# A four-layer decoder kernel: the first layer's cross attention in steps of two heads

## The chip, the cores and the metric

The kernel runs on one core of a Trainium2 chip, as one program. The metric is the device time of one execution in microseconds. Five engines work side by side and meet through semaphores: TensorE (PE, with its weight loads shown apart as PEld), VectorE (DVE), ScalarE (ACT), GpSimd (POOL) and SyncE (SP), which only issues DMAs. Each engine works through its own instructions in order.

## The reference

Sixteen sequences of 112 tokens with 256 features go through four layers, each with self attention (or a state-space block) and cross attention to a context of 375 rows. All is float32. What matters here is the second half of the first layer, cut to its core:

```
# D, H, DH = 256, 16, 64; x: (16, 112, 256), context: (16, 375, 256)
xn, cn = layer_norm(x, gamma_ca), layer_norm(context, gamma_ctx)
q = heads(xn @ w_q) * DH ** -0.5          # 16 heads of 64
k, v = split(cn @ w_kv)                   # one head of keys and values for all queries
p = softmax(q @ k.T, axis=-1)             # (16 heads, 112, 375) for each sequence
attn = merge_heads(p @ v) @ w_out
ff = (silu(gate) * value) @ w_ff2         # gate, value = split(xn @ w_ff1)
x = x + attn + ff
```

## The kernel before

The layers run one after the other. `layer0` (L814) takes the sequences in pairs: 8 turns, the last one written apart, since it prepares no next pair. Each engine has its own program for a turn (`turn`), written in the same order of steps on all: self attention, a middle part (`between_phases`), cross attention, `turn_ending`. No planner decides anything; the order is written out by hand, with lags.

**Items.** Queries lie with their features on the partitions: heads 2t and 2t+1 in the lower and the upper 64 partitions of `qT[:, j, t, :]`. Seen as rows (`rows_of`), the 8 head pairs of 112 tokens are 896 columns per sequence, cut into 7 tiles of 128. An item of the cross attention is one tile and one side: `cross_at(k)` gives sequence j, tile m and side a, so there are 2 x 7 x 2 = 28 items in a turn, 224 in all, and items k and k+1 (k even) are the two sides of one tile. The keys are kept twice, in `ckz[:, j, 0, :]` with zeros in the upper and in `ckz[:, j, 1, :]` with zeros in the lower 64 partitions. So a score product contracts all 128 partitions (`cross_q`, `cross_k`), and the zeros pick the side.

**Steps of one item** (class `Columns`, L227):

- *scores* (L303, product at L311): TensorE, 128 x 375 into one of two PSUM banks of the ring `S`. A float32 product shows as two MATMUL records.
- *maxima* (L447): VectorE reads the bank and makes the negated maximum of each row.
- *exps* (L409): ScalarE reads the bank, writes the exponentials to a slot of `p` in SBUF, and their sums. The end of it frees the bank.
- *inverses* (L456) and *scale* (L365): VectorE's reciprocal of the sums, and the scaling of `p` in place.
- *turns* (L319): TensorE transposes `p` in three parts of 125 keys into one of two banks of the ring `TR`.
- *turned* (L389): ScalarE copies them into a slot of `pT`.
- *values* (L341): TensorE multiplies by the values, for two items at once: item k-1 into the lower and item k into the upper 64 partitions of an output bank, 6 products in 12 records. Every 8 items or so VectorE copies the output bank (L429).

**Order.** `lagged` (L187) runs a loop over steps n on every engine. At step n TensorE does the turns of item n-3, the scores of item n, and for odd n the values of items n-5 and n-4. ScalarE does the copy of item n-3, then the exponential of item n. VectorE does the maximum of item n, then the inverse and scaling of item n-1, then what output copy is due.

**Beside the attention** each step may have other work (`cross_side`), behind the attention's own on each engine. On TensorE: at steps 0 and 2 the products of the last two gates of the feed-forward (8 records of 128x224), at 3 the values of the second context, at 25 the transposes of the next tokens, at 28 to 30 keys, the output products of the first sequence, values and queries. On ScalarE the tanh of each gate (L1153); on VectorE its hidden part (L1281, L1283), the statistics of the next tokens at step 8 (`measure_x`) and their centring at step 12.

The class has a second way for items whose scores get a bias (`by_probs`, used in the third and the fourth layer). There VectorE takes the scores out of the bank with one custom instruction (L444), which adds the bias, writes the negated sums to `p` and keeps their minimum, and a second record that reads the minimum out. ScalarE then takes the exponential from `p` (L406), with scale -1. The bank is free after VectorE's instruction. Since the custom instruction carries no wait, a memset of one element (`take_wait`, L692) waits ahead of it. The self attention of the first layer (`grouped`) has its own form of this.

Of the kernel before, what the change touches and what calls it, by code (L numbers as in the profile page):

```python
# [9 lines left out]
NB, T, D, S2 = 16, 112, 256, 375  # L10
PAIR = 2
# [188 lines left out]
class Part:  # L200


    def __init__(self, name, items, dh, rows, q, k, val, ready, val_ready, place, out, bias=None, grouped=False, sides=2, tiles=CT,
                 turned_by="act", emptied_by="dve", scaled_by="dve", ring=None):
        self.name, self.items, self.dh, self.rows, self.q, self.k, self.val, self.ready = name, items, dh, rows, q, k, val, ready
        self.val_ready, self.place, self.out, self.bias, self.grouped, self.sides, self.ring = val_ready, place, out, bias, grouped, sides, ring
        self.turned_by, self.emptied_by, self.scaled_by = turned_by, emptied_by, scaled_by
        self.keys, self.tiles = (T, 1) if grouped else (CP, tiles)
        self.n = G if grouped else 1
        self.by_probs = bias is not None  # L210
        self.scored_by = "dve" if self.by_probs else "act"

    def bursts(self, k):
        return self.grouped or k % self.sides == self.sides - 1
# [12 lines left out]
class Columns(Attention):  # L227
# [74 lines left out]
    def tensor(self, pe, i, parts, ident, between=None):  # L302
        S, TR, p, pT = self.S, self.TR, self.p, self.pT  # L303

        def scores(ph, k):
            m = ph.first + k
            for sem, count in S.free(i, m, *ph.ready(k)):
                pe.wait_ge(sem, count)
            width = ph.keys * ph.tiles
            for g in range(ph.n):  # L310
                last = pe.matmul(S.bank(m)[:ph.rows, g * width:(g + 1) * width], ph.q(k, g), ph.k(k, g), start=True, stop=True)  # L311
            last.then_inc(S.full.sem, 1)

        def turns(ph, k):
            m = ph.first + k
            for sem, count in TR.free(i, m, self.scaled[ph.scaled_by].this(ph.scaled0 + k)):
                pe.wait_ge(sem, count)
            for g in range(ph.n * ph.tiles):
                last = pe.transpose(TR.bank(m)[:ph.keys, g * ph.rows:(g + 1) * ph.rows], p[:ph.rows, m % self.p_slots, g * ph.keys:(g + 1) * ph.keys],  # L319
                                    ident[:ph.rows, :ph.rows])  # L320
            last.then_inc(TR.full.sem, 1)

        def values(ph, k):
            if not ph.bursts(k):
                return
            m, P, w = ph.first + k, ph.ring or self.P, ph.rows
            job, column = ph.place(k)
            together = [k] if ph.grouped else list(range(k - ph.sides + 1, k + 1))
            ready = [TR.got(ph.first + n) for n in together] + ph.val_ready(k)
            for sem, count in P.free(i, job, *ready) if ph.opens(k) else counts(i, *ready):  # L330
                pe.wait_ge(sem, count)
            bank = P.bank(job)
            if ph.grouped:
                for g in range(ph.n):
                    a, c = g % ph.sides, g // ph.sides
                    last = pe.matmul(bank[a * ph.dh:(a + 1) * ph.dh, c * w:(c + 1) * w], ph.val(k, g, 0), pT[:ph.keys, m % self.pT_slots, g * w:(g + 1) * w],
                                     start=True, stop=True)
            else:
                for t in range(ph.tiles):
                    for a, n in enumerate(together):  # L340
                        last = pe.matmul(bank[a * ph.dh:(a + 1) * ph.dh, column:column + w], ph.val(n, 0, t),  # L341
                                         pT[:ph.keys, (ph.first + n) % self.pT_slots, t * w:(t + 1) * w], start=(t == 0), stop=(t == ph.tiles - 1))
            last.then_inc(P.full.sem if ph.closes(k) else self.values.sem, 1)

        self.lagged(parts, [(self.lag_t, turns), (0, scores), (self.lag_v, values)], between)
# [39 lines left out]
    def scalar(self, act, i, parts, between=None, amid=None):  # L385
        S, p, nm, sums = self.S, self.p, self.nm, self.sums
# [23 lines left out]

        def turned(ph, k):
            if ph.turned_by == "act":
                self.turned_copy(act, i, ph, k, copy)

        def outputs(ph, k):
            if ph.emptied_by == "act" and ph.closes(k):
# [8 lines left out]
    def vector(self, dve, i, parts, between=None, amid=None):  # L425
        S, p, nm, sums, rs = self.S, self.p, self.nm, self.sums, self.rs
# [32 lines left out]

        def turned(ph, k):  # L460
            if ph.turned_by == "dve":
                self.turned_copy(dve, i, ph, k, copy)

        def outputs(ph, k):
            if ph.emptied_by == "dve" and ph.closes(k):
# [348 lines left out]
def layer0(nc, c, x_in, context, x_out, lines, w, prefetch, next_x):  # L814


    DH, HT = 64, H * 64 // 128
# [3 lines left out]
    with ctx:  # L821
        def sb(name, *shape):
            return ctx.enter_context(nc.sbuf_tensor("l0_" + name, list(shape), F32))
# [7 lines left out]
        ktmp, kz = sb("ktmp", 128, 2, TP), sb("kz", 128, PAIR, 2, T)  # L831
# [3 lines left out]
        OT = sb("OT", 128, PAIR, 8, T)  # L835
        cx, cT = sb("cx", CP, PAIR, CT, D), sb("cT", 128, PAIR, KT, S2)
        ckz, cv = sb("ckz", 128, PAIR, 2, S2), sb("cv", CP, PAIR, CT, DH)
        st, mv = sb("st", 128, 6, 6), sb("mv", 128, 3, 6, 2)
        ve, rstd = sb("ve", 128, 6), sb("rstd", 128, 3, 6)
        cos, sin = c.rope[:, 0:TP], c.rope[:, TP:2 * TP]  # L840
# [12 lines left out]
        rows_of = qT[:, :, :, :].rearrange("p j n t -> p j (n t)")  # L853
        OT_of = OT[:, :, :, :].rearrange("p j n t -> p j (n t)")
        LAG_VALUES = 4
        ROWS, TILES = 128, HT * T // 128
# [14 lines left out]
        def cross_at(k):  # L871
            return k // (2 * TILES), k % (2 * TILES) // 2, k % 2
# [9 lines left out]

        def cross_q(k, g):
            j, m, a = cross_at(k)
            return rows_of[:, j, ROWS * m:ROWS * (m + 1)]

        def cross_place(k):
            j, m, a = cross_at(k)
# [2 lines left out]
        def cross_out(k):  # L891
# [3 lines left out]
        own = Part("s", PAIR * H // G, DH, T, own_q, lambda k, g: kz[:, own_at(k)[0], g % 2, :], lambda k, g, t: v[:, own_at(k)[0], :], own_ready, own_values_ready,  # L895
                   lambda k: (f"sO{own_at(k)[0]}{own_at(k)[1]}", 0), lambda k: OT_of[:, own_at(k)[0], own_at(k)[1] * 2 * T:(own_at(k)[1] + 1) * 2 * T],
                   bias=lambda k: wide(c.causal[:T, :], 1, G), grouped=True, scaled_by="pool")
        cross = Part("c", PAIR * 2 * TILES, DH, ROWS, cross_q, lambda k, g: ckz[:, cross_at(k)[0], cross_at(k)[2], :], lambda k, g, t: cv[:, cross_at(k)[0], t, :],
                     cross_ready, cross_values_ready, cross_place, cross_out)

        beside_own = {s: [(f"f{s}", "dve")] for s in range(8)}
        beside_own[8] = [("cT00", "act"), ("cT01", "act"), ("y0", "dve")]
# [61 lines left out]
        def _(pool):  # L964
# [18 lines left out]
            for s in (rooted, pool_steps.raises):  # L983
                pool.sem_inc(s.sem, COMING)
            A.scaled["pool"].prime(pool)
            for a in (kz[:, :, :, :], ckz[:, :, :, :]):
                pool.memset(a, 0.0).then_inc(zeroed, 1)
            pool.wait_ge(zeroed, 2)
            pool_steps.start(-1, COMING)
# [260 lines left out]
        def _(dve):  # L1250
# [9 lines left out]
            def center(i, n, sources, outs):  # L1260
                m, size = NORMS.index(n), sources[0].shape[0]
                dve.wait_ge(rooted.sem, rooted.count(i, m))
                for a, (src, out) in enumerate(zip(sources, outs)):
                    last = dve.tensor_scalar(out, src, mv[:size, m, a, 0:1], rstd[:size, m, a:a + 1], ALU.subtract, ALU.mult)
                last.then_inc(normed.sem, 1)
# [119 lines left out]
            lines.scale(dve, banks[0:2])  # L1385
            measure_context(-1)
            center(-1, "c", context_rows, context_rows)
            with dve.Fori(0, TURNS - 1) as i:
                turn(i, True)
            turn(TURNS - 1, False)  # L1390
# [1979 lines left out]
```

## Time and profile before

| | us |
|---|---|
| median of 3 runs | 3669.17 (3668.32 to 3670.8) |
| the profiled execution | 3673.39 |
| its span | 3671.6 |
| TensorE busy | 3435.7 (94%) |
| TensorE weight loads | 2524.7 (69%) |
| ScalarE busy | 1912.8 (52%) |
| VectorE busy | 1881.6 (51%) |
| GpSimd busy | 397.5 (11%) |

The span is what the profile covers of the execution. Busy times are unions of an engine's records; matmuls are pipelined, so that a record (0.48 us for 128x375) is longer than the time from one start to the next. For TensorE the times from start to start are the ones to add up. In a timeline, instructions of one kind that follow each other are one row: start, length of the whole, engine, line, operation, output and input, count, and in brackets the idle time ahead of it with what ended it.

### The profile page before, as it was taken

Reading aid. Unit: us, or ns where it says so; the run is one execution under the profiler, and the core shown is the slowest. Engines: PE = TensorE matmul, PEld = TensorE weight load, DVE = VectorE, ACT = ScalarE, POOL = GpSimd, SP = SyncE. Lnnn points to the kernel's source line nnn. Section 1 sums busy time; section 2 is a strip of 40 time slices with the busy share of each in tenths; the row PEclk is TensorE's granted clock in tenths of the full one; section 3 lists DMA queues with packets and bytes.
Section 4 is the critical chain, followed back from the end, with each engine's and each line's share of the span. In section 5 each row is a group of like instructions: output and inputs, shape, how many; then the busy total and the mean of one; then the engine's idle time right before and its main releaser. Section 6 shows DMA issues by size and latency. Waiting matters only on the chain. (4 is left out here: it accounts for less than half of the span.)

```text
span 3671.6 us, 67713 instructions
## 1 busy us (share of the span) xinstructions
PE 3435.7 (94%) x21748; PEld 2524.7 (69%) x21748; DVE 1881.6 (51%) x5735; ACT 1912.8 (52%) x5549; POOL 397.5 (11%) x488
## 2 busy tenths in 40 slices
PE   8999999999997999999988999999999998798887
PEld 6778778778775666666656666667666675565665
DVE  3654654644644444455544554455445444656655
ACT  3553543544544555656644554555555454366666
POOL 2101101101102111001101000000000000211111
PEclk9999999999998999999999999999999999899999
DMA  6000000000004000000001000000000000000000
GB/s 207 4 12 15 4 12 15 4 12 15 4 3 150 14 8 5 13 13 13 13 6 55 9 8 11 8 12 9 8 15 9 8 10 14 12 18 22 13 27 5
DMA packets 58462, 75.11 MB, mean 20 GB/s; under 512 B 6752, under 2 KB 55584, under 8 KB 57024
## 3 DMA queue, kind: packets, MB, share of 16 engines
q1 hardware_dynamic: 58176, 71.45, 6.3%
q8 instruction: 160, 2.62, 0.3%
q14 instruction: 126, 1.03, 0.1%
HBM read 64.04 MB, written 7.40 MB: 19 GB/s over the span
## 5 line engine op out<-in xcount | busy, mean ns | idle before, releaser
L161 PE MATMUL l_bank<-l_xT,weights_of_layers_and 128*128 128x224 f32 x2816 | 616.7, 371 | 14.8 <-ACT l_xT L1143 8.0
L161 PEld LDWEIGHTS l_bank<-l_xT,weights_of_layers_and 128*128 128x128 f32 x2816 | 542.4, 199 | 58.4 <-ACT l_xT L1143 8.7
L389 ACT ACTIVATE l_pT<-l_bank 125x336 f32<-125x336 f32 (+2 forms) x736 | 347.6, 472 | 321.1 <-PE l_bank L319 310.8
L319 PEld LDWEIGHTS l_bank<-identity,l_p 112*125 112x125 f32 (+2 forms) x2336 | 332.1, 177 | 198.6 <-issue 112.0
L319 PE MATMUL l_bank<-identity,l_p 112*125 112x112 f32 (+2 forms) x2336 | 387.7, 278 | 36.2 <-ACT l_p L363 30.8
L406 ACT ACTIVATE l_p<-l_p,l_nm 112x375 f32<-112x375 f32 x384 | 233.2, 607 | 234.3 <-DVE l_nm L444 233.0
L161 PE MATMUL l_bank<-weights_of_layers_and,l_cT 128*125 128x256 f32 (+2 forms) x960 | 303.8, 454 | 13.6 <-DVE l_queries_or_hidden L1845 9.3
L161 PE MATMUL l_bank<-l_cT,weights_of_layers_and 128*128 128x375 f32 x832 | 304.0, 494 | 0.0
L710 POOL TENSOR_TENSOR l_ve<-l_mv,eps 112x2 f32<-112x2 f32 (+1 forms) x89 | 17.3, 195 | 2438.8 <-DVE l_mv L704 2438.8
L402 ACT ACTIVATE l_p<-l_p,l_nm 112x112 f32<-112x112 f32 x512 | 192.2, 377 | 149.4 <-DVE l_nm L440 130.8
L341 PEld LDWEIGHTS l_bank<-l_pT,l_cv 125*64 125x64 f32 (+1 forms) x3648 | 162.8, 130 | 137.0 <-issue 97.0
L444 DVE CUSTOM_DVE_ANT_0 l_p<-l_bank,weights_of_layers_and 112x375 f32<-112x375 f32 x256 | 139.3, 544 | 202.4 <-issue 122.0
L161 PEld LDWEIGHTS l_bank<-weights_of_layers_and,l_cT 128*125 128x125 f32 x960 | 160.4, 189 | 101.0 <-issue 53.6
L341 PE MATMUL l_bank<-l_pT,l_cv 125*64 125x112 f32 (+2 forms) x3648 | 225.0, 272 | 2.0 <-ACT l_pT L389 1.8
L161 PEld LDWEIGHTS l_bank<-l_cT,weights_of_layers_and 128*128 128x128 f32 x832 | 155.2, 194 | 100.2 <-issue 16.3
L365 DVE TENSOR_SCALAR l_p<-l_p,l_rs 112x375 f32<-112x375 f32 (+1 forms) x480 | 199.5, 416 | 17.1
L311 PE MATMUL l_bank<-l_ckT,l_qz 128*112 128x375 f32 x512 | 203.2, 480 | 0.2
L640 DVE TENSOR_REDUCE l_nm<-l_bank 112x1 f32<-112x375 f32 x256 | 140.1, 547 | 123.4 <-PE l_bank L554 121.3
L554 PE MATMUL l_bank<-l_ckT,l_queries_or_hidden 128*112 128x375 f32 x512 | 201.2, 479 | 0.0
L562 PEld LDWEIGHTS l_bank<-identity,l_p 112*125 112x125 f32 (+1 forms) x1024 | 140.2, 175 | 85.0 <-ACT l_p L619 27.8
L562 PE MATMUL l_bank<-identity,l_p 112*125 112x112 f32 (+1 forms) x1024 | 171.3, 280 | 7.8 <-ACT l_pT L623 5.6
L409 ACT ACTIVATE l_p<-l_bank,l_nm 128x375 f32<-128x375 f32 x224 | 128.5, 574 | 96.1 <-DVE l_nm L447 95.4
(255 smaller groups left out, 5887.4 us busy)
## 6 DMA issues: line engine op xcount, KB each, us to landing
l_cT<-in_ctx_turned SPq DMA_DIRECT2D x32, 375.0 KB, 3.5
l_cx<-in_ctx SPq DMA_DIRECT2D x16, 375.0 KB
context_rows<-in_ctx_reversed SPq DMA_DIRECT2D x16, 375.0 KB
tokens<-x_after_layer SPq DMA_DIRECT2D x25, 224.0 KB, 2.5
x_after_layer<-l_z SPq DMA_DIRECT2D x24, 224.0 KB, 2.4
weights_of_layers_and<-bias_lines_kept SPq DMA_DIRECT2D x1, 2625.0 KB, 15.6
weights_of_layers_and<-in_L_xattn_w_fused SPq DMA_DIRECT2D x1, 2048.0 KB, 10.9
weights_of_layers_and<-in_L_xattn_w_ff SPq DMA_DIRECT2D x1, 2048.0 KB, 12.8
```

The source lines that it names most:

```text
L161: last = pe.matmul(out, left, right, start=(k == 0), stop=(k == len(pairs) - 1))
L311: last = pe.matmul(S.bank(m)[:ph.rows, g * width:(g + 1) * width], ph.q(k, g), ph.k(k, g), start=True, stop=True)
L319: last = pe.transpose(TR.bank(m)[:ph.keys, g * ph.rows:(g + 1) * ph.rows], p[:ph.rows, m % self.p_slots, g * ph.keys:(g + 1) * ph.keys], i ...
L341: last = pe.matmul(bank[a * ph.dh:(a + 1) * ph.dh, column:column + w], ph.val(n, 0, t), pT[:ph.keys, (ph.first + n) % self.pT_slots, t * w ...
L365: eng.tensor_scalar(own, own, self.rs[:r, c:c + 1], None, ALU.mult).then_inc(self.scaled["dve"].sem, 1)
L389: return act.activation(out, src, ACT.Copy)
L402: last = act.activation(own, own, ACT.Exp, bias=nm[:r, c + g:c + g + 1], accum_out=sums[:r, c + g:c + g + 1])
L406: act.activation(own, own, ACT.Exp, bias=nm[:r, c:c + 1], scale=-1.0, accum_out=sums[:r, c:c + 1]).then_inc(self.probs.sem, 1)
L444: dve.tensor_tensor_reduce(p[:r, m % self.p_slots, 0:S2], S.bank(m)[:r, 0:S2], ph.bias(k), -1.0, 3.0e38, ALU.add, ALU.min, nm[:r, c:c + 1] ...
L554: last = pe.matmul(S.bank(m)[:T, g * width:(g + 1) * width], ph.q(k, g), ph.k(k, g), start=True, stop=True)
L562: last = pe.transpose(TR.bank(m)[:ph.keys, g * T:(g + 1) * T], p[:, m % self.p_slots, g * ph.keys:(g + 1) * ph.keys], ident[:T, :T])
L640: dve.tensor_reduce(nm[:, n, k:k + 1], S.bank(m)[:T, 0:S2], AX.X, ALU.max, negate=True).then_inc(self.neg_max.sem, 1)
```

## The change

The cross attention of the first layer goes in steps of two items. Each product contracts only the 64 partitions that hold its side (`cross_q` and the new `cross_k`). On TensorE the scores of items n and n+1 are issued together at even n, behind the waits of both, and the turns of two items together at even n; ScalarE's copies are paired in the same way. The part gets a bias of zeros, so it now takes the `by_probs` way: VectorE takes the scores out, ScalarE's exponential reads SBUF. GpSimd fills the zeros at the start. Other parts keep `abreast=1`, which issues what was issued before.

```diff
+    def abreast_of(self, k):
+        n = self.abreast
+        return range(k - n + 1, k + 1) if k % n == n - 1 else ()
...
         def scores(ph, k):
-            m = ph.first + k
-            for sem, count in S.free(i, m, *ph.ready(k)):
-                pe.wait_ge(sem, count)
+            own = ph.abreast_of(k + ph.abreast - 1)
             width = ph.keys * ph.tiles
-            for g in range(ph.n):
-                last = pe.matmul(S.bank(m)[:ph.rows, g * width:(g + 1) * width], ph.q(k, g), ph.k(k, g), start=True, stop=True)
-            last.then_inc(S.full.sem, 1)
+            for n in own:
+                for sem, count in S.free(i, ph.first + n, *ph.ready(n)):
+                    pe.wait_ge(sem, count)
+            for n in own:
+                for g in range(ph.n):
+                    last = pe.matmul(S.bank(ph.first + n)[:ph.rows, g * width:(g + 1) * width], ph.q(n, g), ph.k(n, g), start=True, stop=True)
+                last.then_inc(S.full.sem, 1)
 
         def turns(ph, k):
-            m = ph.first + k
-            for sem, count in TR.free(i, m, self.scaled[ph.scaled_by].this(ph.scaled0 + k)):
-                pe.wait_ge(sem, count)
...
+            for n in ph.abreast_of(k):
+                m = ph.first + n
+                for sem, count in TR.free(i, m, self.scaled[ph.scaled_by].this(ph.scaled0 + n)):
+                    pe.wait_ge(sem, count)
...
         def turned(ph, k):
             if ph.turned_by == "act":
-                self.turned_copy(act, i, ph, k, copy)
+                for n in ph.abreast_of(k):
+                    self.turned_copy(act, i, ph, n, copy)
...
+        no_bias = sb("no_bias", 128, S2)
...
         def cross_q(k, g):
             j, m, a = cross_at(k)
-            return rows_of[:, j, ROWS * m:ROWS * (m + 1)]
+            return rows_of[64 * a:64 * a + 64, j, ROWS * m:ROWS * (m + 1)]
+
+        def cross_k(k, g):
+            j, m, a = cross_at(k)
+            return ckz[64 * a:64 * a + 64, j, a, :]
...
-        cross = Part("c", PAIR * 2 * TILES, DH, ROWS, cross_q, lambda k, g: ckz[:, cross_at(k)[0], cross_at(k)[2], :], lambda k, g, t: cv[:, cross_at(k)[0], t, :],
-                     cross_ready, cross_values_ready, cross_place, cross_out)
+        cross = Part("c", PAIR * 2 * TILES, DH, ROWS, cross_q, cross_k, lambda k, g, t: cv[:, cross_at(k)[0], t, :],
+                     cross_ready, cross_values_ready, cross_place, cross_out, bias=lambda k: no_bias[:, :], abreast=2)
...
-            for a in (kz[:, :, :, :], ckz[:, :, :, :]):
+            for a in (kz[:, :, :, :], ckz[:, :, :, :], no_bias[:, :]):
                 pool.memset(a, 0.0).then_inc(zeroed, 1)
...
+            dve.wait_ge(zeroed, 3)
             with dve.Fori(0, TURNS - 1) as i:
```

## Rows read from the trace of the kernel before

**Rows 1.** Windows of the first layer's cross attention, one turn; columns in the first line.
```profile
core 0: us, PE busy (x) PEld busy (x) DVE busy (x) ACT busy (x) POOL busy (x), PEclk, DMA share, GB/s
367.70:424.70 57.00, 56.77 (x398) 41.50 (x397) 35.87 (x107) 32.91 (x94) 0.89 (x2) 1.00 0.00 1
```

**Rows 2.** Timeline of TensorE in that stretch: start, length, engine, line, names, count.
```profile
376.93 0.88 PE L341 MATMUL l_bank<-l_pT,l_cv 125*64 125x128 f32 x12
377.74 0.59 PE L319 MATMUL l_bank<-identity,l_p 128*125 128x128 f32 x3
378.17 0.80 PE L311 MATMUL l_bank<-l_ckz,l_qT 128*128 128x375 f32 x2
378.80 0.49 PE L319 MATMUL l_bank<-identity,l_p 128*125 128x128 f32 x3
379.13 0.80 PE L311 MATMUL l_bank<-l_ckz,l_qT 128*128 128x375 f32 x2
379.85 0.88 PE L341 MATMUL l_bank<-l_pT,l_cv 125*64 125x128 f32 x12
```

**Rows 3.** Timeline of ScalarE and VectorE in the same stretch.
```profile
398.34 0.48 ACT L389 ACTIVATE l_pT<-l_bank 125x384 f32<-125x384 f32 x1
398.75 0.57 ACT L409 ACTIVATE l_p<-l_bank,l_nm 128x375 f32<-128x375 f32 x1
...
400.11 0.55 DVE L447 TENSOR_REDUCE l_nm<-l_bank 128x1 f32<-128x375 f32 x1 [0.87 <-PE l_bank L311]
```

**Rows 4.** Timeline of the fourth layer: scores taken out with a bias.
```profile
3182.42 0.48 PE L311 MATMUL l_bank<-l_ckT,weights_of_layers_and 128*112 128x375 f32 x1
...
3183.04 0.06 DVE L692 MEMSET l_scratch<- 1x1 f32 x1 [0.48 <-PE l_bank L311]
...
3183.57 0.16 DVE L456 RECIPROCAL l_rs<-l_sums 112x1 f32<-112x1 f32 x1
...
3183.69 0.61 ACT L406 ACTIVATE l_p<-l_p,l_nm 112x375 f32<-112x375 f32 x1 [0.54 <-DVE l_nm L444]
```

**Rows 5.** Timeline of VectorE at the third layer's end: reciprocal, scaling, memset.
```profile
3088.71 0.16 DVE L456 RECIPROCAL l_rs<-l_sums 112x1 f32<-112x1 f32 x1
3088.90 0.41 DVE L365 TENSOR_SCALAR l_p<-l_p,l_rs 112x375 f32<-112x375 f32 x1
3089.26 0.06 DVE L692 MEMSET l_scratch<- 1x1 f32 x1
```

**Rows 6.** Timeline of the start of the first layer's cross attention.
```profile
364.68 3.19 PE L161 MATMUL l_bank<-l_xT,weights_of_layers_and 128*128 128x224 f32 x16
...
367.71 0.79 PE L311 MATMUL l_bank<-l_ckz,l_qT 128*128 128x375 f32 x2
367.99 0.36 ACT L1153 ACTIVATE l_th<-l_bank 128x224 f32<-128x224 f32 x1 [1.16 <-PE l_bank L161]
...
369.11 0.54 DVE L447 TENSOR_REDUCE l_nm<-l_bank 128x1 f32<-128x375 f32 x1
...
375.24 0.80 PE L311 MATMUL l_bank<-l_ckz,l_qT 128*128 128x375 f32 x2
```

**Rows 7.** Timeline around steps 8, 12 and 24 of the same stage.
```profile
382.58 0.42 DVE L365 TENSOR_SCALAR l_p<-l_p,l_rs 128x375 f32<-128x375 f32 x1
...
383.86 0.52 DVE L447 TENSOR_REDUCE l_nm<-l_bank 128x1 f32<-128x375 f32 x1
...
389.22 0.73 DVE L1264 TENSOR_SCALAR l_xhat<-tokens,l_mv,l_rstd 112x256 f32<-112x256 f32 x2
...
405.12 0.80 PE L311 MATMUL l_bank<-l_ckz,l_qT 128*128 128x375 f32 x2
```

**Rows 8.** Timeline: TensorE where it starts again, turns and values.
```profile
384.48 0.42 DVE L365 TENSOR_SCALAR l_p<-l_p,l_rs 128x375 f32<-128x375 f32 x1
...
385.04 0.56 PE L319 MATMUL l_bank<-identity,l_p 128*125 128x128 f32 x3 [0.23 <-DVE l_p L365]
...
3664.46 0.45 ACT L389 ACTIVATE l_pT<-l_bank 125x336 f32<-125x336 f32 x1 [0.38 <-PE l_bank L319]
...
3664.96 0.49 PE L341 MATMUL l_bank<-l_pT,l_cv 125*32 125x112 f32 x11 [0.60 <-ACT l_pT L389]
```

More of the change, by code:

```diff
@@ L203, in __init__ @@
     def __init__(self, name, items, dh, rows, q, k, val, ready, val_ready, place, out, bias=None, grouped=False, sides=2, tiles=CT,
-                 turned_by="act", emptied_by="dve", scaled_by="dve", ring=None):
+                 turned_by="act", emptied_by="dve", scaled_by="dve", ring=None, abreast=1):
+        self.abreast = abreast
         self.name, self.items, self.dh, self.rows, self.q, self.k, self.val, self.ready = name, items, dh, rows, q, k, val, ready
@@ L305, in scores @@
         def scores(ph, k):
-            m = ph.first + k
-            for sem, count in S.free(i, m, *ph.ready(k)):
-                pe.wait_ge(sem, count)
+            own = ph.abreast_of(k + ph.abreast - 1)
             width = ph.keys * ph.tiles
-            for g in range(ph.n):
-                last = pe.matmul(S.bank(m)[:ph.rows, g * width:(g + 1) * width], ph.q(k, g), ph.k(k, g), start=True, stop=True)
-            last.then_inc(S.full.sem, 1)
-        def turns(ph, k):
-            m = ph.first + k
-            for sem, count in TR.free(i, m, self.scaled[ph.scaled_by].this(ph.scaled0 + k)):
-                pe.wait_ge(sem, count)
[L318 to L321, printed above, removed]
+            for n in own:
[5 more added lines that the diff above has]
+                last.then_inc(S.full.sem, 1)
+        def turns(ph, k):
+            for n in ph.abreast_of(k):
+                m = ph.first + n
+                for sem, count in TR.free(i, m, self.scaled[ph.scaled_by].this(ph.scaled0 + n)):
+                    pe.wait_ge(sem, count)
+                for g in range(ph.n * ph.tiles):
+                    last = pe.transpose(TR.bank(m)[:ph.keys, g * ph.rows:(g + 1) * ph.rows], p[:ph.rows, m % self.p_slots, g * ph.keys:(g + 1) * ph.keys],
+                                        ident[:ph.rows, :ph.rows])
+                last.then_inc(TR.full.sem, 1)
         def values(ph, k):
@@ L461, in turned @@
             if ph.turned_by == "dve":
-                self.turned_copy(dve, i, ph, k, copy)
+                for n in ph.abreast_of(k):
+                    self.turned_copy(dve, i, ph, n, copy)
         def outputs(ph, k):
```

## The prediction

> **What bounds the kernel now.** I read the page first: TensorE is busy for 94% of the span, the other engines for about half. Then the windows of the stretch that the change touches, the cross attention of the first layer: of the 57 us that it takes in one turn, 56.77 us are TensorE work, at a granted clock of 1.00, while VectorE has 35.9 us and ScalarE 32.9 us [rows 1]. Then the timeline of TensorE. A pair of heads (items m and m+1) costs it 2.92 us. Two score products take 0.63 us each (378.17 to 378.80), two groups of turns 0.43 and 0.33 (377.74 to 378.17, 378.80 to 379.13), the values 0.81 with the change of mode behind them (376.93 to 377.74), and the change ahead of them 0.09 (0.72 from 379.13 to the values of the next pair, less 0.63): 1.26 + 0.76 + 0.81 + 0.09 = 2.92 [rows 2]. Nothing waits on TensorE. VectorE sits idle for 0.87 us ahead of a reduce, until a score product ends [rows 3]. So TensorE is the bound, and there are 14 pairs in each of 8 turns. The question is whether it stays the bound.
>
> **Scores on half the rows.** Each item's product now contracts 64 partitions, one item on the lower and one on the upper half, into two banks. No row shows two products in different row halves. Below, they overlap wholly, and a pair costs 0.63; above, not at all, 1.26. The nearest rows are the values, which sit in two column halves: 12 records take 0.81 including the change, where 12 records of the turns' rate (0.33 for 3) would take 1.32 [rows 2]. They overlap in twos, so I take 0.63.
>
> The Trainium skill (TensorE: Matmul & The Clock Gate, Part 3) has such products run side by side at about 4 ns each. That is the same 0.63, so by it the sum stands.
>
> The change of mode into the row halves is new. It lies between nothing and the whole 0.35 that a change into and out of the column halves costs (0.09 ahead, 0.81 less 6 x 0.11 behind, and 0.10 on the first turn). I take 0.15 into it, and keep 0.09 into the values. TensorE's own work per pair becomes 0.76 + 0.15 + 0.63 + 0.09 + 0.81 = 2.44, 0.48 less than now.
>
> **The new order.** TensorE issues turns(m-4), turns(m-3), scores(m), scores(m+1), values(m-4, m-3). Before, turns and scores alternated, and values(m-4, m-3) came after turns(m-2) and scores(m+1). There are still two score banks, and the scores of a pair wait until both are free. ScalarE issues copy(m-4), copy(m-3), exp(m), exp(m+1), VectorE take(m), inverse(m-1), take(m+1), inverse(m). A take is a memset, the custom add-and-minimum and its accumulator read; an inverse is reciprocal and scaling.
>
> **The takes.** The last score's start plus its 0.48 gives its end; the memset starts 0.14 later, for 3182.42 + 0.48 = 3182.90 against 3183.04. The next VectorE instruction starts 0.53 after the memset, and the exponential of that item 0.65 after it, so a take is over at 0.61 [rows 4]. An inverse holds VectorE for 0.55 (3088.71 to 3089.26) [rows 5]. The exponential from SBUF holds ScalarE for 0.61 [rows 4], a copy for 0.41 (398.34 to 398.75), with 0.48 to its end [rows 3]. VectorE has 2 x (0.53 + 0.55) = 2.16 of work per pair and ScalarE 2 x (0.61 + 0.41) = 2.04. By busy time alone everyone fits under 2.44. The order is what does not.
>
> The Trainium skill (TensorEngine Tiling (Array Packing), PSUM Bottleneck) warns that tiling speeds up TensorE but not the emptying of PSUM, and that both engines should share the emptying. By that rule this change, which gives the scores to VectorE alone, would gain less than 0.48 a pair; the loops below are how that would look here.
>
> **Two loops.** The short one goes through the banks. From take(m+1) over: TensorE restarts (0.15, as a turn after a scaling: 384.48 + 0.42 to 385.04 [rows 8]), change 0.15, scores 0.32 + 0.48 = 0.80, then 0.14 + 0.53 for take(m+2), 0.55 for inverse(m+1), 0.61 for take(m+3): 2.93 for one pair. The long one goes through the copies, since on ScalarE the copies of m-2 and m-1 are queued behind exp(m+1). From take(m+1) over: 0.04 + 0.61 for the exponential, 0.41 + 0.48 for two copies, 0.05 to the values (3664.46 + 0.45 to 3664.96 [rows 8]), values 0.81, turns(m), turns(m+1) 0.76, change 0.15, scores 0.80, and 0.14 + 0.53 + 0.55 + 0.61 until take(m+5) is over. That is 5.94 for two pairs, 2.97 each. Behind the values wait the turns and the scores of the pair after. So what ended last, TensorE at 2.92, is replaced by a chain of 2.97, and TensorE idles for about half a microsecond per pair. From pair 4 to pair 26 there are 11 steps: 11 x 0.05 = +0.55 us per turn.
>
> **Start of the stage.** At steps 0 and 2 the last two gate products of the feed-forward stand beside the attention. On VectorE their hidden part is queued behind take(0) and ahead of take(1), and scores(2) and (3) now need take(1). The chain is: scores 0.63, back to full rows 0.20 (between nothing and the 0.26 behind the values), gate products 1.51 (half of the 16 from 364.68 to 367.71), 0.28 until the tanh, 1.12 from the tanh to VectorE's next instruction, take(1) 0.61, restart and change 0.30 [rows 6]. That is 4.65, and the same again with step 2, so scores(4) start 9.30 after scores(0). Now it is 7.53 (367.71 to 375.24) [rows 6]. The loss is +1.77 us per turn. Until now TensorE went on with scores(1) while VectorE did the hidden part.
>
> **Insertions on VectorE.** The statistics of the next tokens at step 8 push the next instruction on the scores from 0.36 after a scaling (3088.90 to 3089.26) to 1.28 (382.58 to 383.86), so +0.92; the centring at step 12 holds VectorE for 0.73 [rows 5, 7]. Now TensorE absorbs most: from scores(4) to scores(24) it takes 29.88 us (375.24 to 405.12), 10 x 2.92 and 0.68 more [rows 6, 7]. In the new order both lie inside the loops, 1.65 in place of 0.68: +1.0 us in the seven turns that have a next one. The output copies fall into the time in which VectorE waits for scores; nothing for them. The transposes of the next tokens at step 25 cost TensorE the same on both sides.
>
> **At nothing:** the fill of the zero bias (0.2 to 0.5 us of GpSimd at the very start, ahead of a wait that ends on VectorE), the third count that VectorE waits for once, and the end of the turn, where 7 us of output products on TensorE cover what is late. If that cover is short, it costs 0.3 per turn.
>
> **The sum.** 8 x (0.55 + 1.77) + 7 x 1.0 = 18.6 + 7.0 = +25.6 us. The profiled execution took 3673.39 (span 3671.6 and 1.8 around it), so 3699.0 in its terms; it was 4.2 above the median of the runs, 3669.17, so the median should come to 3694.8, that is 3695 us.
>
> **Rivals.**
> *The row halves don't overlap* (0.15). TensorE then needs 2.44 + 0.63 = 3.07 per pair, above both loops: 11 x 0.10 more than forecast, and 2 x 0.63 in the chain of the start, 2.4 per turn, +19: 3714. For it: fp32 products come as two passes, and no row proves row halves. Against it: the column halves of the values.
> *TensorE stays the bound* (0.12), the one that ends faster. It decides at 2.44: the long loop would have to be under 4.88, 1.06 less than my rows give, for instance if exponentials, copies and restarts overlap more behind one another. Then 11 x 0.48 = 5.3 less; the start at TensorE's own 6.99 (2 x (0.63 + 0.15 + 0.20) + 2 x 1.51 + 1.25 for the context values + 0.76) instead of 7.53; insertions hidden, 0.68 less: 6.5 per turn, -52: 3617. For it: 2.16 and 2.04 of work under 2.44. Against: every link of the long loop has a row, and four of them (exponential, copies, values, turns) are long ones in a fixed order.
> *Gain and loss cancel* (0.09). The mode changes cost nothing and the gates at the start are half hidden: 2.8 per pair gives -1.3, the start +0.9, the insertions +0.5: 3669 to 3670.
> *The clock falls* (0.03). TensorE would wait for a sixth of the stage with half its rows idle. Its 2.44 at the 1.2 GHz level would be near 4.9, against 2.92: 2 x 14 x 8 = +220, 3890. Against: the clock stays at 1.00 wherever this stage waits now.
>
> **Numbers.** My forecast has 0.61, with its own range 3682 to 3710: both loops move by 0.08 a pair with the mode change, the start by 0.4 a turn. The range 3660 to 3722 leaves out the faster rival, the clock and the upper part of the first rival. No change is within 0.2% (7 us), which is what a measurement of this kernel can tell. Faster: 0.12 and a fifth of the third rival, 0.14. Same: the rest of the third, 0.07. Slower: 0.79.
>
> **What would show it.** Right: pairs of score records of 128x375 with the stationary from 64 rows starting within 0.02 us of each other; a pair step of 2.9 to 3.1 us, TensorE idle ahead of the values until a ScalarE copy, and ahead of scores(2) and (4) until VectorE's take; exponentials in the first layer from SBUF at 0.61 us; scores(0) to scores(4) near 9.3 us; a granted clock of 1.00. Wrong: a pair step near 2.5 with TensorE unbroken; score records one behind the other; or a stage under 57 us in one turn.

## The result, and the profile after

The kernel after takes 3684.27 us (median of 7 runs, 3682.54 to 3684.64), the kernel before 3671.07 beside it (7 runs, 3668.32 to 3672.28). The ratio is 1.0035, with a 95% interval of 1.0024 to 1.0046: slower by 13.2 us. The profiled execution took 3684.27 with a span of 3682.5, 10.9 more than the span before, at a mean granted clock of 0.977 (before 0.976).

The page has TensorE busy for 92% of the span in place of 94%: it now has less to do, and waits instead.

Windows of the kernel after in the first layer: a whole turn, from its first score product to that of the next turn, then the score products 0 to 26 (the last pair) of one of the first seven turns and of the last.

```profile
core 0: us, PE busy (x) PEld busy (x) DVE busy (x) ACT busy (x) POOL busy (x), PEclk, DMA share, GB/s
371.12:507.47 136.35, 126.01 (x858) 102.81 (x857) 71.90 (x263) 64.44 (x204) 15.88 (x22) 1.00 0.03 11
371.12:413.76 42.64, 35.87 (x290) 24.49 (x289) 30.49 (x144) 27.60 (x77) 0.95 (x2) 1.00 0.01 1
1054.65:1095.48 40.83, 35.44 (x286) 24.17 (x285) 28.90 (x137) 27.61 (x77) 0.00 (x0) 1.00 0.00 1
```

The kernel before, with the same columns: a whole turn, one that is 1.68 longer because the granted clock is lower in it, and the same two stretches of score products.

```profile
367.71:501.55 133.84, 131.16 (x857) 107.01 (x857) 71.37 (x207) 63.87 (x204) 15.79 (x22) 1.00 0.04 11
232.19:367.71 135.52, 132.84 (x857) 108.35 (x856) 71.36 (x207) 63.87 (x204) 15.80 (x22) 0.99 0.03 11
367.71:408.39 40.68, 40.45 (x289) 28.11 (x289) 30.48 (x92) 27.63 (x80) 0.89 (x2) 1.00 0.00 1
1040.43:1080.08 39.65, 39.65 (x285) 28.11 (x285) 28.44 (x85) 27.31 (x79) 0.00 (x0) 1.00 0.00 1
```

Compare turns at the same clock: 133.84 against 136.35, +2.51 us. Between scores(0) and scores(26) TensorE's work fell by 4.58 us (40.45 to 35.87), and the stretch grew by 1.96 (40.68 to 42.64): 6.77 us of the stretch are now idle, where 0.23 were.

Groups of instructions of the first layer in the kernel after: who makes whom wait (busy us, mean ns, then idle time ahead and its releaser).

```profile
L453 DVE CUSTOM_DVE_ANT_0 l_p<-l_bank,l_no_bias 128x375 f32<-128x375 f32 x224 | 121.9, 544 | 68.1 <-PE l_bank L327 37.1 <-issue 30.7
L318 PE MATMUL l_bank<-l_ckz,l_qT 64*128 64x375 f32 x448 | 101.5, 530 | 21.0 <-DVE l_nm L453 21.0
L349 PE MATMUL l_bank<-l_pT,l_cv 125*64 125x128 f32 x1344 | 98.1, 281 | 40.7 <-ACT l_pT L397 38.7 <-issue 0.7
```

TensorE waits twice: 21.0 us ahead of scores, for VectorE's take, and 40.7 us ahead of values, for ScalarE's copy. That is 7.7 us per turn. Both are the waits that the prediction named.

Timeline of the start of the stage after, answering to [rows 6].

```profile
371.12 0.90 PE L318 MATMUL l_bank<-l_ckz,l_qT 64*128 64x375 f32 x4
371.95 1.78 PE L161 MATMUL l_bank<-l_xT,weights_of_layers_and 128*128 128x224 f32 x8
...
374.24 0.39 DVE L1296 SCALAR_TENSOR_TENSOR l_u<-l_th,l_bank 128x224 f32<-128x224 f32 x1 [1.26 <-ACT l_th L1168]
...
374.97 0.54 DVE L453 CUSTOM_DVE_ANT_0 l_p<-l_bank,l_no_bias 128x375 f32<-128x375 f32 x1
375.58 0.90 PE L318 MATMUL l_bank<-l_ckz,l_qT 64*128 64x375 f32 x4 [1.84 <-DVE l_nm L453]
...
380.08 0.90 PE L318 MATMUL l_bank<-l_ckz,l_qT 64*128 64x375 f32 x4
```

VectorE has the instruction that uses the tanh (L1296) queued behind take(0), waits 1.26 us for the tanh, and only then makes take(1), for which TensorE has stood for 1.84 us. scores(0) to scores(4) take 8.96 us (371.12 to 380.08), where they took 7.53 [rows 6].

TensorE some pairs later, after, answering to [rows 2].

```profile
383.58 0.90 PE L318 MATMUL l_bank<-l_ckz,l_qT 64*128 64x375 f32 x4
...
385.22 1.03 PE L327 MATMUL l_bank<-identity,l_p 128*125 128x128 f32 x6
386.18 0.90 PE L318 MATMUL l_bank<-l_ckz,l_qT 64*128 64x375 f32 x4
387.62 0.88 PE L349 MATMUL l_bank<-l_pT,l_cv 125*64 125x128 f32 x12 [0.54 <-ACT l_pT L397]
...
389.75 0.90 PE L318 MATMUL l_bank<-l_ckz,l_qT 64*128 64x375 f32 x4 [0.40 <-DVE l_nm L453]
```

The four passes of two items take 0.90 us to the end of the record, where two passes of one item took 0.80 [rows 2]. The pair steps are 2.60 and 3.57. The second holds VectorE's statistics: TensorE waits 0.40 us for the take that stands behind them.

The loops undisturbed, in the last turn, after. The steps are 2.66 (1078.39 to 1081.05) and 3.04 (to 1084.09), 2.85 on average.

```profile
1080.34 0.54 DVE L453 CUSTOM_DVE_ANT_0 l_p<-l_bank,l_no_bias 128x375 f32<-128x375 f32 x1
1080.92 0.61 ACT L414 ACTIVATE l_p<-l_p,l_nm 128x375 f32<-128x375 f32 x1 [0.30 <-DVE l_nm L453]
1081.05 0.90 PE L318 MATMUL l_bank<-l_ckz,l_qT 64*128 64x375 f32 x4
1081.53 0.85 ACT L397 ACTIVATE l_pT<-l_bank 125x384 f32<-125x384 f32 x2
1081.99 0.54 DVE L453 CUSTOM_DVE_ANT_0 l_p<-l_bank,l_no_bias 128x375 f32<-128x375 f32 x1 [0.58 <-issue]
1082.01 0.06 DVE L702 MEMSET l_scratch<- 1x1 f32 x1
1082.43 0.88 PE L349 MATMUL l_bank<-l_pT,l_cv 125*64 125x128 f32 x12 [0.48 <-ACT l_pT L397]
```

This is the long loop: take until 1080.88, exponential 0.61, two copies 0.85, values, turns. It also shows where the forecast of the takes was too long: scores start at 1081.05 and their records end at 1081.95, the take starts at 1081.99. The record of the memset lies beside it (1082.01), not ahead of it.

### The profile page after: what moved, and what is told of

Read it like the earlier page. It is cut to its first block and busy times, and to the rows that moved or that the text cites. A ratio compares the mean times of both kernels' runs of the same rounds, so it can differ in the third digit from the quotient of the medians.

```text
span 3682.5 us, 67747 instructions
## 1 busy us (share of the span) xinstructions
PE 3390.8 (92%) x21748; PEld 2487.4 (68%) x21748; DVE 1885.3 (51%) x6183; ACT 1918.2 (52%) x5549; POOL 398.4 (11%) x489
## 5 line engine op out<-in xcount | busy, mean ns | idle before, releaser
L414 ACT ACTIVATE l_p<-l_p,l_nm 112x375 f32<-112x375 f32 (+1 forms) x608 | 369.4, 608 | 346.9 <-DVE l_nm L453 341.6
L397 ACT ACTIVATE l_pT<-l_bank 125x336 f32<-125x336 f32 (+2 forms) x736 | 334.6, 470 | 316.3 <-PE l_bank L327 313.8
L327 PEld LDWEIGHTS l_bank<-identity,l_p 112*125 112x125 f32 (+2 forms) x2336 | 318.7, 177 | 167.1 <-issue 106.7
L327 PE MATMUL l_bank<-identity,l_p 112*125 112x112 f32 (+2 forms) x2336 | 370.9, 278 | 34.0 <-ACT l_p L371 30.8
L629 ACT ACTIVATE l_p<-l_bank,l_nm 112x375 f32<-112x375 f32 x256 | 147.0, 574 | 51.4 <-DVE l_nm L650 49.4
## 6 DMA issues: line engine op xcount, KB each, us to landing
weights_of_layers_and<-in_L_xattn_w_fused SPq DMA_DIRECT2D x1, 2048.0 KB, 10.9
weights_of_layers_and<-in_L_xattn_w_ff SPq DMA_DIRECT2D x1, 2048.0 KB, 13.2
```

Of the source, the lines that this page charges most:

```text
L397: return act.activation(out, src, ACT.Copy)
L414: act.activation(own, own, ACT.Exp, bias=nm[:r, c:c + 1], scale=-1.0, accum_out=sums[:r, c:c + 1]).then_inc(self.probs.sem, 1)
L629: act.activation(slot[:, 0:S2], S.bank(m)[:T, 0:S2], ACT.Exp, bias=nm[:, n, k:k + 1], accum_out=sums[:, n, j, h:h + 1]).then_inc(S.emptier ...
```

## The experiments

Each kernel was timed beside the kernel before, which stood at 3670 to 3672 us throughout. "Steps" are the times from scores(0) to scores(2), from there to scores(4) and so on, in a profiled turn that has a next one. For the kernel after they begin 4.46, 4.51. Ratios are to the kernel before, with 95% intervals.

The traces allow a finer comparison than the totals. Of the second to the sixth turn, those in which the granted clock is 1.00 throughout take the same time within 0.03 us in each kernel (but for one turn of the side-work experiment, 1.0 longer). What differs from trace to trace besides the work is the number of short stretches (3.4 us) at half the granted clock, and the time behind the first layer, where the code is the same in all of them. Each row is one profiled execution:

| kernel | turn at full clock, us | stretches at half clock, first layer after 100 us | from the last turn's second output products to the end, us |
|---|---|---|---|
| before | 133.84 | 3 | 2578.1 |
| after | 136.35 | 1 | 2572.8 |
| half rows alone | 140.79 | 4 | 2577.3 |
| pairs, full rows | 136.87 | 1 | 2572.1 |
| take alone | 133.90 | 4 | 2572.0 |
| pairs, no take | 140.47 | 2 | 2574.3 |
| side work odd | 132.36 | 2 | 2575.9 |
| gates odd | 134.03 | 5 | 2574.8 |
| before, side work odd | 133.19 | 0 | 2577.4 |
| turns apart | 133.24 | 0 | 2575.9 |
| both | 130.05 | 1 | 2573.8 |

The last column spreads over 6 us with nothing changed, so a gap of a few microseconds between two profiled executions says nothing about the stage.

### Half rows without the pairs and without the take

The kernel before with only the operands of the score products changed (stationary and moving from 64 rows). Against the kernel after, bias and steps of two are taken out:

```
-                     cross_ready, cross_values_ready, cross_place, cross_out, bias=lambda k: no_bias[:, :], abreast=2)
+                     cross_ready, cross_values_ready, cross_place, cross_out)
```

> The kernel before, with the score products on half the rows and nothing else of the change: one item per step, exponentials from the bank. Theory (order and queues cost, the row halves themselves are sound but give nothing without a partner): each score product stands alone between turns, so it saves nothing and pays a change of mode in and out. After shows 0.85 us from six turns to the scores where six turns at 0.11 are 0.65, and the same behind the values, so about 0.10 for each change and 0.10 for each late first pass: 0.2 to 0.3 per item more, 224 items, +45 to +65 us on 3671, near 3725. Rival (mode changes on the row side are free, since only rows change): 3671, no change.

Measured: 3728.87 us (3726.28 to 3730.63), ratio 1.0154 (1.0137 to 1.0171): +58 us. TensorE in that kernel:

```profile
396.49 0.59 PE L327 MATMUL l_bank<-identity,l_p 128*125 128x128 f32 x3
397.02 0.89 PE L318 MATMUL l_bank<-l_ckz,l_qT 64*128 64x375 f32 x2
397.84 0.59 PE L327 MATMUL l_bank<-identity,l_p 128*125 128x128 f32 x3
398.36 0.90 PE L318 MATMUL l_bank<-l_ckz,l_qT 64*128 64x375 f32 x2
...
399.99 0.59 PE L327 MATMUL l_bank<-identity,l_p 128*125 128x128 f32 x3
```

A product on half the rows between turns on all rows holds TensorE for 0.82 us instead of 0.63, and the turns behind it lose what they had of overlap (0.52 where the second group took 0.33 [rows 2]). A pair takes 3.50 us in place of 2.92, so 0.29 per item goes to the changes between half rows and all rows. By itself, then, the row half is a loss; it pays only where two products share it. The second product of the pair costs nothing: 0.90 us for four passes against 0.89 or 0.90 for two here.

### Pairs and take, scores on all rows

The kernel after without the row halves.

```
-            return rows_of[64 * a:64 * a + 64, j, ROWS * m:ROWS * (m + 1)]
+            return rows_of[:, j, ROWS * m:ROWS * (m + 1)]
-                return ckz[64 * a:64 * a + 64, j, a, :]
+                return ckz[:, j, a, :]
```

> The changed kernel with the products on all 128 rows again (zeros pick the side); pairs and VectorE's takes stay. Theory (two loops through VectorE and ScalarE hold the pair step at 2.6 to 3.1, TensorE waits): the 0.4 us that a pair's scores are longer mostly fill what TensorE waited for, so only +3 to +12 us on 3684, near 3690. Rival (TensorE's own time still decides): 0.43 per pair in 112 pairs, +48, 3732.

Measured: 3689.43 us (3685.98 to 3690.43), ratio 1.0047 (1.0031 to 1.0064), 5 us more than after. TensorE in the middle of a turn:

```profile
400.99 1.43 PE L318 MATMUL l_bank<-l_ckz,l_qT 128*128 128x375 f32 x4
402.35 0.88 PE L349 MATMUL l_bank<-l_pT,l_cv 125*64 125x128 f32 x12
...
403.91 1.43 PE L318 MATMUL l_bank<-l_ckz,l_qT 128*128 128x375 f32 x4
```

Here, undisturbed, TensorE has no wait and the step is 2.92, and still the kernel is 18 us slower than before. The halves, with all that they save on TensorE (2.92 to 2.49), are worth 5 us in this order; pairs and take together cost 18, and the next experiment shows that the take has no part in it. The loss is at the start (4.79, 4.89) and at the insertions (3.45, 3.47).

### The take alone

The kernel before with the zero bias and the take. Against the kernel after, steps of two are taken out, and the operands are on all rows as in the experiment above:

```
-                     cross_ready, cross_values_ready, cross_place, cross_out, bias=lambda k: no_bias[:, :], abreast=2)
+                     cross_ready, cross_values_ready, cross_place, cross_out, bias=lambda k: no_bias[:, :])
```

> The kernel before, with VectorE taking the scores out with the zero bias (exponentials from SBUF) and nothing else: full rows, one item per step. Theory (the take is as long as the maximum, 0.54, and TensorE hides its latency): within 4 us of 3671. Rival (the takes' longer path, memset, accumulator read and exponentials of 0.61, is part of the loss): +8 or more.

Measured: 3665.86 us (3663.67 to 3672.44), ratio 0.9987 (0.9978 to 0.9996): 4.7 us less than the 3670.55 of before beside it, a shade beyond the 4 that were expected. A turn at full clock in it:

```profile
503.31:637.20 133.89, 131.21 (x857) 107.05 (x857) 71.88 (x263) 64.74 (x204) 15.87 (x22) 1.00 0.04 11
```

That is no shorter than the 133.84 before, so the trace does not show that the take gains anything; where the 4.7 come from stays open, and the unchanged code behind the first layer alone differs by 6.1 between the two profiled executions. That VectorE now empties the bank alone costs nothing. So the loss of the change is in the pairs.

### Pairs and halves without the take

The kernel after with the exponential reading the bank again.

```
-                     cross_ready, cross_values_ready, cross_place, cross_out, bias=lambda k: no_bias[:, :], abreast=2)
+                     cross_ready, cross_values_ready, cross_place, cross_out, abreast=2)
```

> The changed kernel without the bias: pairs on half the rows, VectorE makes maxima, ScalarE's exponentials read the banks and free them. Theory: two banks are now held until exp(m+1), and the next scores wait for maximum, exponential and copies: a pair step near 3.2, +30 to +45 on 3684, near 3722; so the takes are what makes pairs bearable. Rival (TensorE's waits come from the order of its own queue, not from who frees the banks): within 6 us of 3684.

Measured: 3727.52 us (3720.89 to 3731.95), ratio 1.0161 (1.0145 to 1.0176), 43 us above after.

```profile
396.75 0.57 ACT L417 ACTIVATE l_p<-l_bank,l_nm 128x375 f32<-128x375 f32 x1 [0.31 <-DVE l_nm L456]
397.32 0.86 ACT L397 ACTIVATE l_pT<-l_bank 125x384 f32<-125x384 f32 x2
397.47 0.90 PE L318 MATMUL l_bank<-l_ckz,l_qT 64*128 64x375 f32 x4 [0.50 <-ACT l_p L417]
```

The scores wait for the second exponential, and the step is 3.21. The take is what makes pairs bearable with two banks: it frees a bank one exponential earlier. The Trainium skill (TensorEngine Tiling (Array Packing), PSUM Bottleneck) advises both engines for the emptying. Here the split version, in which VectorE reduces and ScalarE then reads the same bank, is the slower one by 43 us: both engines on one bank, one behind the other, is not the sharing that helps. That holds for pairs in two banks; with one item per step the two ways take the same time per turn (133.84 and 133.89).

### Side work of VectorE ahead of the other item

In the kernel after, VectorE's side work moves from the even steps to the odd ones. It then stands behind both takes of a pair instead of between them.

```
-                if s in (0, 2):
+                if s in (1, 3):
-                elif coming and s == 8:
+                elif coming and s == 9:
-                elif coming and s == 12:
+                elif coming and s == 13:
```

> The changed kernel with VectorE's side work one step later: the hidden part of the two gates at steps 1 and 3, statistics at 9, centring at 13, so that it stands behind the take of the pair's second item and not ahead of it. Theory: the scores of the next pair are no longer held by it; 1.8 us of the first pair's 1.84 us wait go, and most of the 1.0 us at steps 8 and 12: 2.5 to 3.7 us per turn, -20 to -30 on 3684, near 3658. Rival (the start is lost to the pair order itself, whatever VectorE does beside it): within 4 us of 3684.

Measured: 3657.50 us (3654.33 to 3659.47), ratio 0.9962 (0.9948 to 0.9976): 27 us less than after, and 3.99 less in a turn at full clock. TensorE at the start of the stage there:

```profile
360.99 0.90 PE L318 MATMUL l_bank<-l_ckz,l_qT 64*128 64x375 f32 x4
...
363.54 0.90 PE L318 MATMUL l_bank<-l_ckz,l_qT 64*128 64x375 f32 x4
...
368.04 0.90 PE L318 MATMUL l_bank<-l_ckz,l_qT 64*128 64x375 f32 x4
```

scores(2) follow scores(0) after 2.55 us, unbroken, and scores(4) after 7.05. The wait of the scores for the take, 21.0 us in the groups of the first layer, is gone; the one of the values for the copies is still there (33.6 against 40.7):

```profile
L318 PE MATMUL l_bank<-l_ckz,l_qT 64*128 64x375 f32 x448 | 101.0, 527 | 0.0
L349 PE MATMUL l_bank<-l_pT,l_cv 125*64 125x128 f32 x1344 | 98.1, 281 | 33.6 <-ACT l_pT L397 32.0 <-issue 0.4
```

### Only the gates' hidden part moved

```
-                if s in (0, 2):
+                if s in (1, 3):
```

> The changed kernel with only the hidden parts of the two gates one step later (1 and 3); statistics and centring stay at 8 and 12. It splits the 27 us of the side work. Theory: the first pair step falls from 4.46 to 2.54, 1.9 us in each of 8 turns, and the third from 3.50 towards 3.1: -15 to -18 on 3684, near 3668, that is the kernel before; the rest of the 27 belongs to the statistics. Rival (one delay hides the other, so the steps at 8 and 12 grow by what the start gains): within 6 us of 3684.

Measured: 3670.11 us (3665.73 to 3674.1), ratio 0.9996 (0.9987 to 1.0006), 14 us less than after, a little short of the 15 to 18 that were expected. By the medians that is half of the 27. The start saves 1.92 per turn (8.97 to 7.05), 15.4 in 8 turns. This trace has five stretches at half clock where the kernel after has one; at full clock a turn is 2.32 shorter than after (136.35 to 134.03), so the gates have nearer six tenths of the 3.99. The wait of the scores in the first layer is 9.6 us, and what is left of it comes from steps 8 and 12.

### The same move in the kernel before

```
-                if s in (0, 2):
+                if s in (1, 3):
-                elif coming and s == 8:
+                elif coming and s == 9:
-                elif coming and s == 12:
+                elif coming and s == 13:
```

> The kernel before with VectorE's side work at odd steps (1, 3, 9, 13) and nothing else, as a fair rival to e5. Theory: the kernel before loses only what it showed at steps 8 and 12, 0.47 and 0.19 us in seven turns, so -3 to -5 us: 3667. If it fell by 25 as the changed one did, the side work and not the pairs would be what e3 showed.

Measured: 3660.91 us (3659.4 to 3667.09), ratio 0.9978 (0.9969 to 0.9987): 9.6 us less than the 3670.55 beside it, where 3 to 5 were expected. One turn of it:

```profile
362.59:495.78 133.19, 130.76 (x857) 107.32 (x857) 71.03 (x207) 64.05 (x204) 15.83 (x22) 1.00 0.04 11
```

133.19 against 133.84 at the same clock is 0.65 per turn, 4.6 in seven turns, as expected. The rest of the 9.6 is not settled. The clock is one candidate: in the kernel before, three turns of the first layer after the first 100 us hold a stretch of 3.4 us at half the granted clock and last some 1.65 us more (135.52 against 133.84 above); this kernel has none, and 3 x 1.65 = 5.0. But that is one trace of each kernel, and these two profiled executions differ by 12.5, of which 2.0 lie ahead of the first cross attention, where the edit changes nothing (the first scores start at 98.22 before and at 96.22 here). What the experiment does tell apart: the move is worth up to 10 us in the kernel before, and 27 in the kernel after; in a turn at full clock, 0.65 against 3.99. So two thirds or more of the 27 are a fault of the new order.

### Turns and copies one item at a time

In the kernel after the scores stay in pairs; turns and their copies go back to single steps.

```
-            for n in ph.abreast_of(k):
+            for n in (k,):
```

(in the turns on TensorE and in their copies on ScalarE and VectorE, three places)

> The changed kernel with the turns and ScalarE's copies one item per step again, as before; the scores stay paired on half the rows. Theory (the long loop, exponential of m+1, two copies, values, is what makes TensorE wait 0.5 to 0.9 us ahead of the values): the first copy runs a step earlier, ahead of the exponential, and the values find both copies done; the pair step goes to 2.7 against 2.87 at one more change of mode: 1.5 to 3 us per turn, -12 to -24, near 3664. Rival (the waits move elsewhere, the added change of mode, 0.2 us a pair, is all that is seen): +22, 3706.

Measured: 3658.11 us (3655.36 to 3662.97), ratio 0.9966 (0.9957 to 0.9976): 26 us less than after, a little more than the 12 to 24 that were expected. Groups of its first layer, and a timeline of TensorE:

```profile
L318 PE MATMUL l_bank<-l_ckz,l_qT 64*128 64x375 f32 x448 | 101.0, 527 | 23.6 <-DVE l_nm L453 23.6
L349 PE MATMUL l_bank<-l_pT,l_cv 125*64 125x128 f32 x1344 | 98.1, 281 | 0.9 <-ACT l_pT L397 0.6
```

```profile
374.48 0.90 PE L318 MATMUL l_bank<-l_ckz,l_qT 64*128 64x375 f32 x4
375.31 0.59 PE L327 MATMUL l_bank<-identity,l_p 128*125 128x128 f32 x3
375.83 0.88 PE L349 MATMUL l_bank<-l_pT,l_cv 125*64 125x128 f32 x12
...
377.16 0.90 PE L318 MATMUL l_bank<-l_ckz,l_qT 64*128 64x375 f32 x4
```

The mirror image of the side-work experiment: the wait of the values for the copies is gone (40.7 to 0.9), the one of the scores for the take stays (21.0 to 23.6). The undisturbed step is 2.68, one change of mode more than 2.49 but with no wait. So the long loop was what bounded the undisturbed pair, and it ran through the two copies queued behind exp(m+1).

### Both

Both edits in the kernel after.

> Side work at odd steps and turns one item per step together. Theory (two separate loops, each relieved by one of the edits): the gains of 27 and 26 us overlap only where one wait hid the other; start of the stage 1.8, statistics 1.0 and the copies' waits all go, and TensorE is left with 2.7 per pair and few waits: 3636 to 3642, under both kernels. Rival (both edits relieve the same wait): no better than either, 3655.

Measured: 3632.70 us (3631.48 to 3634.14), ratio 0.9897 (0.9882 to 0.9912): 38 us less than before, 52 less than after. It beats both kernels, and ends a little below what was expected.

```profile
L318 PE MATMUL l_bank<-l_ckz,l_qT 64*128 64x375 f32 x448 | 101.0, 527 | 0.0
L349 PE MATMUL l_bank<-l_pT,l_cv 125*64 125x128 f32 x1344 | 98.1, 281 | 0.6 <-ACT l_pT L397 0.6
```

```profile
366.18 0.90 PE L318 MATMUL l_bank<-l_ckz,l_qT 64*128 64x375 f32 x4
367.01 0.59 PE L327 MATMUL l_bank<-identity,l_p 128*125 128x128 f32 x3
...
368.86 0.90 PE L318 MATMUL l_bank<-l_ckz,l_qT 64*128 64x375 f32 x4
```

Both waits are gone, TensorE is unbroken, and nearly every step is 2.68. The stage is again bound by TensorE, with less for it to do. The two gains nearly add up: 27 + 26 = 53 against 52, and in a turn at full clock 3.99 + 3.11 = 7.10 against 6.30.

## Why the prediction was right, point by point

It said slower, because VectorE's and ScalarE's order would take the place of TensorE as the bound. Both waits are in the trace where it put them, and the experiments take them away one by one. The size was too large: +25.6 forecast, +13.2 measured. At equal clock the first layer lost 19.5 where 25.6 were forecast. That the whole came out as low as 13.2 has to do with the clock and with code that was not changed, which the sum did not have. By its own steps:

- **Row halves overlap: right.** Taken one by one, the first records of the two products of a pair start 7 ns apart, and the pair costs what one product on half rows costs. The rival in which they don't overlap fell. TensorE's own work per pair is 0.84 + 0.80 + 0.85 = 2.49, forecast 2.44. The change of mode into the rows, taken as 0.15, is nearer 0.20 with the late first pass.
- **The loops: the mechanism was right, the size too large.** The long one was put at 5.94 for two pairs and is 5.70: exponential 0.65, copies 0.86, 0.05, values 0.80, turns with change 0.85, scores 0.90, then 0.04 + 0.47 + 0.53 + 0.55. The term that was mis-sized is the last one, from the end of the scores until both takes are over: 0.14 + 0.53 + 0.55 + 0.61 = 1.83 forecast, 1.59 measured. These 0.24 are the whole difference; the other terms miss by up to 0.10 each and cancel. Of the 0.24, 0.10 is the start of the first take, 0.04 behind the score's end and not 0.14. In the fourth layer, from where the 0.14 came [rows 4], the memset does start that late, and the custom instruction another 0.06 later (at 3183.10, a row not shown there); why both are quicker in the new stage, no run shows. So the pair step, a short one of 2.66 and a long one of 3.04, averages 2.85 instead of 2.97. From scores(4) to scores(26) of the last turn, where six of the 11 steps are long ones and the first is 3.29, the average is 2.90, a shade below the old 2.92: the kernel after gains 0.27 where +0.55 was forecast. So the sign of this term was wrong. Undisturbed, the loops bound the stage but cost nothing against the kernel before; the slowdown is all in the start, the insertions and the tail.
- **Start: right, 1.43 instead of 1.77.** The restart behind a take and the change were taken as 0.30; scores start 0.07 behind the take's end (375.51 to 375.58). Shown by moving the gates' hidden part: the start falls to 7.05.
- **Insertions: right, 0.80 instead of 1.0.** It is the 1.96 of a turn with a next one, less the 1.43 of the start, and the 0.27 back.
- **Tail: wrong, 0.5 instead of 0.** From scores(26) to the output products of the second sequence (L1010, after L1025) it is 17.82 us before (408.39 to 426.21) and 18.32 after (413.76 to 432.08). TensorE has 0.43 less to do there but idles for 0.96 us right behind the last scores, ahead of the values, and the output products, which come later, can't cover that. The text had given 0.3 for a short cover.

```profile
415.62 0.88 PE L349 MATMUL l_bank<-l_pT,l_cv 125*64 125x128 f32 x12 [0.96 <-ACT l_pT L397]
```

- **The sum.** 1.43 - 0.27 + 0.80 + 0.5 = 2.5 per turn with a next one, as the 2.51 of the windows; the forecast had 3.3. With the last turn (1.18 up to scores(26) and 0.70 behind), 7 x 2.51 and 1.9, that is 19.5 at equal clock. 3.3 of the difference to 13.2 go with the clock, of which the kernel before had three short stretches at half speed in the first layer and the kernel after one. What is left of it is 3 us by the medians (13.2) and 5 by the profiled executions (10.9). In these it lies behind the first layer: 2578.1 before and 2572.8 after for the same code (last column of the table above). Why such a stretch varies stays open.
- **Clock: right but for one turn.** It stays at 1.00 in the stage though TensorE waits for a sixth of it, in seven turns of eight. In the fourth, the stretch at half clock (from 512.1) falls into the start of the stage, just after TensorE had waited 1.85 us for a take, and scores(0) to scores(4) take 10.61 us:

```profile
507.47:518.08 10.61, 8.76 (x44) 6.54 (x43) 5.37 (x23) 3.25 (x10) 0.00 (x0) 0.84 0.00 1
```

- **TensorE stays the bound: fell for this kernel.** The rival needed the long loop under 4.88. With the turns taken apart and the side work moved TensorE is the bound again, by queue order alone, but at 2.68 a pair; that shows the loop at no more than 5.36 for two pairs, and whether it could go under 4.88 is open.
- **Gain and loss cancel: fell.** It put the loops at -1.3, the start at +0.9 and the insertions at +0.5 per turn, where -0.27, +1.43 and +0.80 were measured. The sign of the loops it had right.

## What to carry to other kernels

When two items are put abreast, each in-order queue has to be gone over again. What stood between the items now stands ahead of the second item, and whoever waits for both waits for it too: here two reorderings of a few lines, each worth 26 or 27 us, turned +13 us into -38. A saving on the bounding engine (0.43 us of 2.92 per pair, up to 48 us in 112 pairs) is worth little, here 5 us, until the next loop, through its waits and queues, is shorter as well; add that loop up link by link before the change is made. And products on half the rows pay only side by side: alone each costs 0.29 us more.

## What the runs showed of the hardware that was not expected

- The record of the memset ahead of a custom VectorE instruction is not always ahead of it: in the new stage the custom instruction starts 0.04 us after the scores' record ends, with the memset's record 0.02 after that. In the fourth layer of the kernel before the memset starts 0.14 after the scores' record and the custom instruction 0.20 after it. What decides between the two, no run shows.
- TensorE starts 0.06 us after the VectorE take that it waited for in 21 of 22 waits of the kernel after (0.15 in the other), where it started 0.15 after a scaling [rows 8].
- Stretches of about 3.4 us at half the granted clock cost 1.3 to 1.7 us each and fell into three turns of the first layer before, one after, and none to five in the other kernels, by one trace of each. What brings them on is not shown. Two kernels a few microseconds apart can differ by these alone.
